# Which engine issues half of the second pass's loads: GpSimd in place of ScalarE, in a graph kernel that reads an 8192 x 8192 matrix twice

## The chip, the cores and the metric

One core of one Trainium2 chip runs the whole kernel. The metric is device time in microseconds (us) of one execution; lower is better. A profile is one further execution, recorded by the hardware profiler. Its durations are those of single instructions as that execution had them. Engines are TensorE (PE), VectorE (DVE), ScalarE (ACT), GpSimd (POOL) and SyncE (SP); a q behind the name (ACTq) is the engine's instruction queue, where DMA issues are seen.

## The reference

```python
x = layernorm(x + (1 - 0.1*x - 0.01 * sum(x * (adj @ x), axis=1)))      # first layer, x is 8192 x 64
A  = adj - diag(diag(adj))                                             # adj is 8192 x 8192 float32
node_support = concat([(A > 0) @ h, (A < 0) @ h])                       # h is the new x
edge_output  = gru_cell(node_support, h, ...)
att = softmax(where(A > 0, e_plus, -9e15) ...)                          # by rows; needs counts and sums of the positive entries
node_output  = gru_cell((att * A) @ (h @ W), h, ...)
out = layernorm(h + diag(adj) * edge_output + diag(adj) * node_output)
```

`adj` is sparse in its values (most entries are zero, the rest positive), but it is stored and read as a dense matrix of 268 MB. The first layer needs one pass over it, the second layer another, since `h` of all rows must be known before any row of the second layer can be done.

## The kernel before

**First pass.** SP streams `adj` in strips of 128 rows x 2048 columns (1 MB each) into a ring of 8 slots in SBUF; PE makes the Gram products, DVE multiplies and sums them (L610), ACT counts signs (L506). Every eighth tile a group of 1024 rows of `h` is finished; it goes to `h_rows` in DRAM and comes back in another layout as `hk` (`store_rows` L267, `rows_back` L276). The last group is finished in the seam between the passes by DVE, in steps that stand between its first transposes (`SEAM`).

**Second pass.** There are K = 16 blocks of 512 rows. A block is read as U = 8 units of 2 MB, and the same ring serves as 4 slots of one unit each (`SLOTS`). A unit is loaded by four DMAs, one for each group g of 32 partitions (`load_unit`, L247): partitions 32g to 32g+31 get columns 2048g + 256u to 2048g + 256u + 255 of the 512 rows. So one DMA moves 512 KB in 512 pieces of 1 KB, 32 pieces for each of the 16 DMA engines. Groups 0 and 1 (partitions 0 to 63) are issued by SP, groups 2 and 3 (partitions 64 to 127) by ACT; for units 0 to 3 of block 0 SP issues all four.

When the four DMAs of a unit have landed, POOL sets the diagonal of `adj` in it to zero (`no_diagonal`, L719). Then DVE transposes it in two halves (L806, `turned`), ACT takes the signs of each half (L932, `mask`, `mask_ready`), and PE multiplies: `weigh` (L1033) with the values, `add` (L1045) with the signs, in pairs of halves. The slot is free as soon as DVE has turned the second half. SP waits for that semaphore alone. ACT comes to its two DMAs in program order, behind the sign of the second half.

The small work of block k-1 (sums, softmax, gates, layer norm, store) is spread over the halves of block k: lists `AT` on each engine say at which half a step stands. On DVE `weighed_sum` (L813) stands at half 3 and `added_sum` (L818) at half 4, `reset` (L853) at half 10, the variance at 15 and `result` (L887) at 16. PE can't begin `weigh` of half 0 of a block before L813, nor `add` of half 0 before L818, since these steps empty its accumulators. POOL does the square root of the layer norm (`power`, L767) after the eighth `no_diagonal` of a block. ACT's steps are at halves 1, 2, 5, 6, 9, 10 and 16, among them three DMAs of 128 KB for each block (L946, L950, L989).

The order on POOL between the passes: it waits for `hk`'s first half, makes the high and low parts of it (L428, L430), and then comes to the first `no_diagonal`.

Of the kernel before, what the change touches and what calls it, by code (L numbers as in the profile page):

```python
# [6 lines left out]
Q = 32  # L7
G = P // Q
# [36 lines left out]
def build_gnn(nc, x, adj, w_gat, a_gat, w_ih_e, w_hh_e, b_ih_e, b_hh_e, w_ih_n, w_hh_n, b_ih_n, b_hh_n, out):  # L45
    N = adj.shape[0]
    GQ = N // G
    C = GQ // Q
    NB = N // P
    assert N % 8192 == 0 and x.shape[1] == D  # L50


    STRIP = 4 * BANK
    SPT = N // STRIP
    RING = 8
    TPB = RING // SPT
    LNG = 8
    GROUPS = C // LNG
    GC = C // 2
    XG = C // 4  # L60


    K = N // BANK
    UC = 8
    U = C // UC
    SLOTS = 4
    HC = UC // 2
    MS = 4
    H = 2 * U
    RB = BANK // Q  # L70


    scratch = nc.dram_tensor("h_rows", (N, D), F32, kind="Internal").ap()
    stack = ExitStack()

    def sem(name):
        return stack.enter_context(nc.semaphore(name))

    def keep(name, shape, dt):
        return stack.enter_context(nc.sbuf_tensor(name, shape, dt))  # L80

    with stack:

        hk = keep("hk", [P, C, D], F32)
        parts = keep("parts", [P, C, 2, D], F32R)
        ring = keep("ring", [P, RING, STRIP], F32)


        at = keep("at", [P, 4, HC, BANK], F32)
        mask = keep("mask", [P, MS, HC, BANK], F32R)
        final = keep("final", [P, 8, BANK], F32)
        ps = stack.enter_context(nc.psum_tensor("ps", [P, 8, BANK], F32))

        ones = keep("ones", [P, P], F32R)
        one = keep("one", [P, 1], F32)
        ident = keep("ident", [P, P], F32)
        flag = keep("flag", [1, 1], I32)
        a12 = keep("a12", [D, 2], F32)  # L100
        wie = keep("wie", [P, 2, 3, D], F32)
        whh = keep("whh", [D, 3, 2 * D], F32)
        w2 = keep("w2", [P, 3, D], F32)
        w_edge = keep("w_edge", [P, 2, D], F32)
        w_node = keep("w_node", [P, 2, D], F32)
        va = keep("va", [P, 2, 2], F32)
        pick = keep("pick", [P, 1], F32)
        two = keep("two", [P, D], F32)
        dnat = keep("dnat", [P, NB], F32)
        bias = keep("bias", [P, 2, 3], F32)  # L110
        brz = keep("brz", [P, 2], F32)
        bhn = keep("bhn", [P, 1], F32)
        not_diag = keep("not_diag", [P, K + U // 2 - 1, Q], F32)
        power = keep("power", [P, LNG], F32)
        keep_x = keep("keep_x", [P, 1], F32)
        lsum = keep("lsum", [P, 4, LNG], F32)


        count = keep("count", [P, C], F32)
        some = keep("some", [P, C], F32)  # L120
        off = keep("off", [P, C], F32)
        zeros = keep("zeros", [P, C], F32)
        dsign = keep("dsign", [P, C], F32)
        nat = keep("nat", [P, 4, D], F32)
        stage = keep("stage", [P, 4, D], F32)
        en = keep("en", [P, 4, 4], F32)
        co = keep("co", [P, 8, 4, 3], F32)
        prob0 = keep("prob", [P, 4, D], F32)
        seen = keep("seen", [P, K * H], F32)
        seen_k = keep("seen_k", [P, K], F32)  # L130
        count_k = keep("count_k", [P, K], F32)
        miss = keep("miss", [1, K + 1], F32)
        ls = keep("ls", [P, 4, 4], F32)


        xn = final[:, :, :].rearrange("p a m -> p (a m)").rearrange("p (c d) -> p c d", d=D)
        x2 = mask[:, :, :, :].rearrange("p s c i -> p (s c i)")
        slot_view = [at[:, i, :, :].rearrange("p c i -> p (c i)") for i in range(4)]
        pair = parts[:, C - 4:C, :, :].rearrange("p c e d -> p (c e d)").rearrange("p (t e m) -> p t e m", t=2, e=2)
        wstage = slot_view[0][:, 4 * P:4 * P + 23 * D].rearrange("p (a d) -> p a d", d=D)  # L140
        signs = slot_view[1].bitcast(BF16).rearrange("p (t m) -> p t m", t=2)
        wT = slot_view[2][0:D, 0:2 * D].rearrange("p (a d) -> p a d", d=D)
        wihn = slot_view[2][0:D, 2 * D:5 * D].rearrange("p (t d) -> p t d", d=D)
        sq = slot_view[3][:, 0:LNG * D].rearrange("p (c d) -> p c d", d=D)
        outer = slot_view[3][:, 512:512 + C * SPT].rearrange("p (c s) -> p c s", s=SPT)
        rowsign = slot_view[3][:, 1024:1024 + C * SPT].rearrange("p (c s) -> p c s", s=SPT)


        hT, tr, tz, hn, nn = (final[:, i, :] for i in (0, 3, 4, 5, 6))
        sums = [final[:, 1, :], at[:, 2, 0, :]]  # L150
        wsum = [final[:, 2, :], at[:, 2, 1, :]]
        y = final[:, 7, 0:4 * D].rearrange("p (b d) -> p b d", d=D)
        yo = final[:, 7, 4 * D:8 * D].rearrange("p (b d) -> p b d", d=D)
        prob = [prob0, at[:, 2, 2, 0:4 * D].rearrange("p (b d) -> p b d", d=D)]
        ysq = hn[:, 0:4 * D].rearrange("p (b d) -> p b d", d=D)
        cnt = [tr, tz]
        lows = nn

        s_carry = sem("carries_waits")
        s_nd = sem("not_diag_made")  # L160
        s_scr = sem("h_stored")
        s_hk = [sem("h_back_even"), sem("h_back_odd")]
        s_hi = [sem("high_first_half"), sem("high_second_half")]
        s_lo = [sem("low_first_half"), sem("low_second_half")]
        s_counts = sem("counts_ready")
        s_dsign = sem("diagonal_signs")
        s_raw = {prefix: [sem(f"{prefix}unit_loaded{i}") for i in range(SLOTS)] for prefix in ("f_", "g_")}
        s_miss, s_missed, s_flag = sem("misses_by_row"), sem("misses"), sem("flag_made")

        b = dict(locals())  # L170
        one_pass(nc, b)
# [67 lines left out]
                full.vector(dve)  # L239


def load_unit(eng, b, prefix, k, u, groups=(0, 1, 2, 3)):

    RB, UC, GQ, slot = b["RB"], b["UC"], b["GQ"], u % b["SLOTS"]
    raw = unit_view(b, slot).rearrange("p (f m) -> p f m", f=RB)
    for g in groups:
        eng.dma_start(  # L247
            raw[Q * g:Q * g + Q, :, :],
            b["adj"][bass.ds(k * BANK, BANK), GQ * g + UC * Q * u:GQ * g + UC * Q * (u + 1)].rearrange(
                "(f ii) m -> ii f m", ii=Q)).then_inc(b["s_raw"][prefix][slot], 16)  # L250


def unit_view(b, slot):
# [49 lines left out]
class First:  # L303
# [22 lines left out]
    def sync(self, sp):  # L326
# [26 lines left out]
        for u in range(b["SLOTS"]):  # L353
            sp.wait_ge(s["gram_free"], 2 + C * SPT - RING + 2 * (u + 1))
            sp.wait_ge(s["signs_summed"], C * SPT - RING + 2 * (u + 1))
            load_unit(sp, b, "f_", 0, u)


    def load_weights(self, pool):
# [352 lines left out]
def no_diagonal(nc, pool, b, prefix, k, u):  # L712

    U, UC, SLOTS = b["U"], b["UC"], b["SLOTS"]
    raw = unit_view(b, u % SLOTS)[:, (u % 2) * UC * (UC * Q):(u % 2 + 1) * UC * (UC * Q)]
    diag = bass.AP(tensor=raw.tensor, offset=raw.offset, ap=[list(raw.ap[0]), [UC * Q + Q, UC], [1, Q]])
    pool.wait_ge(b["s_raw"][prefix][u % SLOTS], (k * (U // SLOTS) + u // SLOTS + 1) * (16 * G))
    carry(pool, b["s_carry"])
    return nc.gpsimd.tensor_tensor(  # L719
        out=diag, in0=diag,  # L720
        in1=b["not_diag"][:, bass.ds(k + (U // 2 - 1 - u // 2), 1), :].to_broadcast([P, UC, Q]), op=ALU.mult)
# [6 lines left out]
class Fast:  # L728
# [33 lines left out]
    def gpsimd(self, pool):  # L762
        nc, b, s = self.nc, self.b, self.s

        def power(k):
            pool.wait_ge(s["variance_ready"], k + 1)
            nc.gpsimd.tensor_tensor(out=b["ls"][:, 3, :], in0=b["ls"][:, 2, :], in1=b["power"][:, 0:4],  # L767
                                    op=ALU.pow).then_inc(s["rstd_ready"], 1)

        def block(k, first):  # L770
            for u in range(self.U):
                no_diagonal(nc, pool, b, "f_", k, u).then_inc(s["diagonal_out"], 1)
                if first and u == 1:
                    self.first.last_power(pool)

        block(0, True)
        self.first.count_rows(pool)
        with pool.Fori(1, self.K) as k:
            block(k, False)
            power(k - 1)  # L780
        power(self.K - 1)


# [132 lines left out]
    def scalar(self, act):  # L916
# [8 lines left out]
        def sign(k, half, first, last):  # L925
            n = k * H + half
            act.wait_ge(s["turned"], n + 1)
            if not (first and half < MS):
# [4 lines left out]
                b["mask"][:, half % MS, :, :].rearrange("p c i -> p (c i)"),  # L933
                b["at"][:, half % 4, :, :].rearrange("p c i -> p (c i)").bitcast(U32), ACT.Sign,
                accum_out=b["seen"][:, bass.ds(n, 1)]).then_inc(s["mask_ready"], 1)
            u = half // 2 + SLOTS
            if half % 2 == 1 and (u < U or not last):
                load_unit(act, b, "f_", k + u // U, u % U, (2, 3))

        def staged_rows(k, first):  # L940

# [535 lines left out]
```

## Time and profile before

| | |
|---|---|
| median of 3 runs | 1680.99 us (1678.02 to 1808.76) |
| the profiled execution | 1673.49 us, of which 1671.7 us from the first instruction to the last |
| second pass | from about 695 us; TensorE starts block 0 at 698 us |
| moved by DMA | 550.18 MB, mean 329 GB/s |
| PE, DVE, ACT, POOL busy | 86%, 82%, 70%, 11% of the span |

The profile gives busy time of engines, not whether that work was in the way of the end. What one stage is limited by is read from who waits for whom in that stage, and from what a queue or an engine does in the gaps.

### The profile page before, as it was taken

Reading aid. Unit: us, or ns where it says so; the run is one execution under the profiler, and the core shown is the slowest. Engines: PE = TensorE matmul, PEld = TensorE weight load, DVE = VectorE, ACT = ScalarE, POOL = GpSimd, SP = SyncE. Lnnn points to the kernel's source line nnn. Section 1 sums busy time; section 2 is a strip of 40 time slices with the busy share of each in tenths; the row PEclk is TensorE's granted clock in tenths of the full one; section 3 lists DMA queues with packets and bytes.
Section 4 is the critical chain, followed back from the end, with each engine's and each line's share of the span. In section 5 each row is a group of like instructions: output and inputs, shape, how many; then the busy total and the mean of one; then the engine's idle time right before and its main releaser. Section 6 shows DMA issues by size and latency. Waiting matters only on the chain.

```text
span 1671.7 us, 22680 instructions
## 1 busy us (share of the span) xinstructions
PE 1445.0 (86%) x6262; PEld 794.9 (48%) x6262; DVE 1368.0 (82%) x1335; ACT 1163.8 (70%) x1409; POOL 178.0 (11%) x226
## 2 busy tenths in 40 slices
PE   7987878887888888558998899899999899999995
PEld 6655656555555555224444444444444444444442
DVE  5999899898989898647878877887788788778874
ACT  6987979797979797436666666666566666666662
POOL 2000000000001010201101111110111011111100
PEclk9999999999999999779999999999999999999996
DMA  9999999999999999999999999999999999999980
GB/s 264 418 421 422 410 422 409 421 410 421 411 421 413 419 413 419 233 200 333 303 288 306 292 293 296 308 288 291 299 305 298 299 302 295 297 300 310 293 215 11
DMA packets 366090, 550.18 MB, mean 329 GB/s; under 512 B 71024, under 2 KB 333184, under 8 KB 333296
## 3 DMA queue, kind: packets, MB, share of 16 engines
q1 hardware_dynamic: 190672, 408.49, 70.5%
q10 hardware_dynamic: 174976, 141.05, 33.1%
q0 software_dynamic: 416, 0.36, 0.1%
q8 instruction: 7, 0.11, 0.0%
q14 instruction: 19, 0.16, 0.0%
HBM read 545.66 MB, written 4.19 MB: 329 GB/s over the span
## 4 chain that ended last, share of the span: by engine, by line
DMA 30%; issue 21%; ACTq 15%; DVE 15%; PE 9%; ACT 7%; SPq 2%; DVEq 1%; POOL 0%; POOLq 0%
DMA ring<-in_adj 18%; ACTq L247 12%; DMA h_rows<-final 11%; DVE at L806 7%; DVE ps L610 5%; ACT mask L932 5%; PE ps L572 5%; SPq L247 2%; PE ps L1033 2%; ACTq L950 1%; PE ps L539 1%; ACTq L946 1%; PE ps L1045 1%; ACTq L989 0%; ACT final L970 0%
## 5 line engine op out<-in xcount | busy, mean ns | idle before, releaser
L932 ACT ACTIVATE mask<-at 128x2048 fp32r<-128x2048 uint32 x256 | 489.4, 1913 | 281.2 <-DVE at L806 189.6
L572 PE MATMUL ps<-mask,parts 128*128 128x512 f32 x2048 | 552.0, 413 | 101.9 <-DVE ps L610 68.2
L610 DVE SCALAR_TENSOR_TENSOR ps<-ring,ps 128x2048 f32<-128x2048 f32 x256 | 584.3, 2301 | 55.3 <-PE ps L572 34.8
L806 DVE STREAM_TRANSPOSE at<-ring 128x2048 f32<-128x2048 f32 x256 | 577.8, 2290 | 43.6 <-POOL ring L719 37.9
L1033 PE MATMUL ps<-at,hk 128*64 128x512 f32 x2048 | 495.6, 620 | 79.7 <-DVE final L813 42.3
L506 ACT ACTIVATE at<-ring 128x2048 bf16<-128x2048 f32 x256 | 488.7, 1909 | 97.0 <-DMA ring<-in_adj 52.5
L572 PEld LDWEIGHTS ps<-mask,parts 128*128 128x128 f32 x2048 | 374.9, 193 | 278.8 <-DVE ps L610 203.8
L1033 PEld LDWEIGHTS ps<-at,hk 128*64 128x64 f32 x2048 | 148.7, 141 | 346.1 <-issue 250.8
L1045 PE MATMUL ps<-mask,parts 128*128 128x512 f32 x1024 | 270.2, 405 | 13.6 <-ACT final L959 12.9
L1045 PEld LDWEIGHTS ps<-mask,parts 128*128 128x128 f32 x1024 | 182.1, 188 | 152.1 <-issue 73.4
L719 POOL TENSOR_TENSOR ring<-ring,not_diag 128x256 f32<-128x256 f32 x128 | 93.8, 733 | 715.0 <-DMA ring<-in_adj 715.0
L853 DVE SCALAR_TENSOR_TENSOR final<-final 128x512 f32<-128x512 f32 x16 | 11.1, 692 | 94.9 <-ACT final L976 89.7
L411 POOL TENSOR_TENSOR at<-at,lsum 128x512 f32<-128x512 f32 x7 | 7.3, 1045 | 435.2 <-DVE lsum L627 435.2
L506 ACT ACTIVATION_READ_ACCUMULATOR at<-ring 128x1 f32 x256 | 48.0, 188 | 0.0
L932 ACT ACTIVATION_READ_ACCUMULATOR mask<-at (+1 forms) x256 | 47.9, 187 | 0.0
L959 ACT COPY final<-ps 64x512 f32<-64x512 f32 x16 | 9.3, 583 | 47.1 <-issue 45.7
L818 DVE TENSOR_TENSOR final<-ps,final 64x512 f32<-64x512 f32 x16 | 10.9, 683 | 35.5 <-ACT final L959 35.5
L610 DVE DVE_READ_ACCUMULATOR ps<-ring,ps (+1 forms) x256 | 36.3, 142 | 0.0
L1079 PE MATMUL ps<-final,w_edge 128*64 128x512 f32 x64 | 35.4, 635 | 0.0
L1080 PE MATMUL ps<-final,w_node 128*64 128x512 f32 x64 | 35.4, 635 | 0.0
L767 POOL TENSOR_TENSOR ls<-ls,power 128x4 f32<-128x4 f32 x16 | 16.2, 1010 | 144.9 <-DVE ls L882 144.9
L968 ACT COPY final<-ps 128x512 f32<-128x512 f32 x16 | 9.4, 587 | 29.0 <-issue 29.0
(152 smaller groups left out, 645.4 us busy)
## 6 DMA issues: line engine op xcount, KB each, us to landing
ring<-in_adj SPq DMA_DIRECT2D x256, 1024.0 KB, 16.2
ring<-in_adj SPq DMA_DIRECT2D x264, 512.0 KB, 10.7
ring<-in_adj ACTq DMA_DIRECT2D x248, 512.0 KB, 14.3
stage<-h_rows ACTq DMA_DIRECT2D x16, 128.0 KB, 16.3
nat<-h_rows ACTq DMA_DIRECT2D x16, 128.0 KB, 15.8
out<-final ACTq DMA_DIRECT2D x16, 128.0 KB, 15.4
h_rows<-final ACTq DMA_DIRECT2D x7, 256.0 KB, 22.7
hk<-h_rows ACTq DMA_DIRECT2D x7, 256.0 KB, 23.9
```

The source lines that it names most:

```text
L247: eng.dma_start(raw[Q * g:Q * g + Q, :, :], b["adj"][bass.ds(k * BANK, BANK), GQ * g + UC * Q * u:GQ * g + UC * Q * (u + 1)].rearrange("(f ...
L506: nc.scalar.activation(signs[:, unit % 2, :], ring[:, unit % RING, :], ACT.Sign, accum_out=row_signs[:, unit:unit + 1]).then_inc(s["signs_ ...
L539: last = nc.tensor.matmul(ps[D * half:D * half + D, q % 4, P * i:P * i + P], xn[:, 4 * q + i, :], ident[:], start=True, stop=True, skip_gr ...
L572: last = nc.tensor.matmul(ps[:, 4 * (n % 2) + i, :], pair[:, t % 2, e, :], x2[:, cols], start=e == 0, stop=e == 1)
L610: nc.vector.scalar_tensor_tensor(out=gram, in0=ring[:, i % RING, :], scalar=1.0, in1=gram, op0=ALU.mult, op1=ALU.mult, accum_out=flat[:, b ...
L719: return nc.gpsimd.tensor_tensor(out=diag, in0=diag, in1=b["not_diag"][:, bass.ds(k + (U // 2 - 1 - u // 2), 1), :].to_broadcast([P, UC, Q ...
L806: nc.vector.transpose(b["at"][:, half % 4, :, :].rearrange("p c (f q) -> p f c q", q=Q), raw[:, :, HC * part:HC * part + HC, :]).then_inc( ...
L932: nc.scalar.activation(b["mask"][:, half % MS, :, :].rearrange("p c i -> p (c i)"), b["at"][:, half % 4, :, :].rearrange("p c i -> p (c i) ...
L1033: last = mm(o, h[:, c, :], b["at"][:, half % 4, cl, :], start=c < 2, stop=c >= H * HC - 2)
L1045: last = mm(ps[:, ACC_S, :], parts[:, c, :], b["mask"][:, half % MS, cl, :], start=c == 0, stop=c == H * HC - 1)
L1079: mm(ps[lo, bank, :], b["w_edge"][:, t, :], sums, start=True, stop=True)
L1080: mm(ps[hi, bank, :], b["w_node"][:, t, :], wsum, start=True, stop=True, skip_group_check=True).then_inc(s["gates"], 1)
```

## The change

GpSimd issues groups 2 and 3 of every unit of the second pass, those of units 0 to 3 of block 0 included. Their completion counts on semaphores of their own (`s_pooled`). GpSimd's order in a block becomes: `no_diagonal(u)`, then a wait until unit u-1 has been turned by DVE, then the two DMAs of unit u+3, then `no_diagonal(u+1)`. The two DMAs leave ACT's program (`sign`). SP issues only groups 0 and 1, of the first four units too. For those four GpSimd issues its eight DMAs in a row before the first `no_diagonal`, but behind the high and low parts of `hk`. The last block is written out apart from GpSimd's loop, so that nothing is loaded behind the matrix's end.

```diff
-def load_unit(eng, b, prefix, k, u, groups=(0, 1, 2, 3)):
+def load_unit(eng, b, prefix, k, u, groups=(0, 1, 2, 3), loaded=None):
+    loaded = loaded or b["s_raw"][prefix]
...
-                "(f ii) m -> ii f m", ii=Q)).then_inc(b["s_raw"][prefix][slot], 16)
+                "(f ii) m -> ii f m", ii=Q)).then_inc(loaded[slot], 16)
...
@@ First.sync, the first four units
-            load_unit(sp, b, "f_", 0, u)
+            load_unit(sp, b, "f_", 0, u, (0, 1))
...
@@ no_diagonal
-    pool.wait_ge(b["s_raw"][prefix][u % SLOTS], (k * (U // SLOTS) + u // SLOTS + 1) * (16 * G))
+    turn = k * (U // SLOTS) + u // SLOTS + 1
+    if prefix == "f_":
+        pool.wait_ge(b["s_raw"][prefix][u % SLOTS], turn * (16 * 2))
+        carry(pool, b["s_carry"])
+        pool.wait_ge(b["s_pooled"][u % SLOTS], turn * (16 * 2))
+    else:
+        pool.wait_ge(b["s_raw"][prefix][u % SLOTS], turn * (16 * G))
...
@@ Fast.gpsimd
-        def block(k, first):
+        def upper(k, u):
+
+            load_unit(pool, b, "f_", k, u, (2, 3), b["s_pooled"])
+
+        def block(k, first, last=False):
             for u in range(self.U):
                 no_diagonal(nc, pool, b, "f_", k, u).then_inc(s["diagonal_out"], 1)
+                v = u + b["SLOTS"] - 1
+                if (not first or u) and (v < self.U or not last):
+                    pool.wait_ge(s["turned"], k * self.H + 2 * u)
+                    carry(pool, b["s_carry"])
+                    upper(k + v // self.U, v % self.U)
                 if first and u == 1:
                     self.first.last_power(pool)
 
+        strips = self.first.UNITS * b["GROUPS"] - b["RING"]
+        for u in range(b["SLOTS"]):
+            pool.wait_ge(self.first.s["gram_free"], 2 + strips + 2 * (u + 1))
+            pool.wait_ge(self.first.s["signs_summed"], strips + 2 * (u + 1))
+            upper(0, u)
         block(0, True)
         self.first.count_rows(pool)
-        with pool.Fori(1, self.K) as k:
+        with pool.Fori(1, self.K - 1) as k:
             block(k, False)
             power(k - 1)
+        block(self.K - 1, False, True)
+        power(self.K - 2)
         power(self.K - 1)
...
@@ Fast.scalar, sign
-            u = half // 2 + SLOTS
-            if half % 2 == 1 and (u < U or not last):
-                load_unit(act, b, "f_", k + u // U, u % U, (2, 3))
```

## Rows read from the trace of the kernel before

**Rows 1.** The page: busy time by engine, GB/s in 40 slices of 41.8 us

```profile
PE 1445.0 (86%) x6262; PEld 794.9 (48%) x6262; DVE 1368.0 (82%) x1335; ACT 1163.8 (70%) x1409; POOL 178.0 (11%) x226
...
GB/s 264 418 421 422 410 422 409 421 410 421 411 421 413 419 413 419 233 200 333 303 288 306 292 293 296 308 288 291 299 305 298 299 302 295 297 300 310 293 215 11
```

**Rows 2.** Stretch A:B, length, busy PE PEld DVE ACT POOL, PEclk, DMA share, GB/s

```profile
1220.00:1340.00 120.00, 111.64 (x522) 52.20 (x521) 97.29 (x95) 76.76 (x87) 14.42 (x19) 1.00 1.11 297
```

**Rows 3.** Who waited for whom, 860 to 1580 us: us in total, times, longest

```profile
POOL ring L719 <- DMA ring<-in_adj: 539.8, 88, 9.8
...
DVE final L853 <- ACT final L976: 77.2, 13, 7.1
...
PE ps L1033 <- DVE final L813: 32.8, 12, 2.8
...
PE ps L1045 <- ACT final L959: 9.7, 6, 1.9
```

**Rows 4.** Instructions in order of time, ACT and DVE, 1319 to 1331 us

```profile
1322.38 2.87 ACTq L247 DMA_DIRECT2D ring<-in_adj  x1
1325.49 1.91 ACT L932 ACTIVATE mask<-at 128x2048 fp32r<-128x2048 uint32 x1 [4.29 <-issue]
...
1328.86 0.69 DVE L853 SCALAR_TENSOR_TENSOR final<-final 128x512 f32<-128x512 f32 x1 [6.80 <-ACT final L976]
```

**Rows 5.** Instructions in order of time, PE, a block's end and start

```profile
1352.84 1.09 PE L1054 MATMUL ps<-ident,stage 128*64 128x128 f32 x16
1356.76 5.07 PE L1033 MATMUL ps<-at,hk 128*64 128x512 f32 x16 [2.83 <-DVE final L813]
```

**Rows 6.** POOL's power step, once a block: ns min/median/max, first and last start

```profile
L767 POOL TENSOR_TENSOR ls<-ls,power x15: 1007/1009/1027, 825.0 to 1633.4; 128x4 f32<-128x4 f32 x15
```

**Rows 7.** Two short stretches of second pass: busy PE, PEclk, DMA share, GB/s

```profile
756.00:762.00 6.00, 6.00 (x28) 1.00 1.10 348
...
1335.00:1339.00 4.00, 4.00 (x23) 1.00 1.12 194
```

**Rows 8.** DMA queues (packets, MB, share) in 690:702, then 712:718, then 764:780

```profile
q1 hardware_dynamic: 2531, 2.51, 102.7%
...
q1 hardware_dynamic: 754, 0.74, 67.0%
q10 hardware_dynamic: 528, 0.53, 45.3%
...
q1 hardware_dynamic: 2783, 2.77, 55.2%
q10 hardware_dynamic: 2786, 2.77, 54.9%
```

**Rows 9.** DMA queue and issues in the first pass, 60 to 640 us

```profile
q1 hardware_dynamic: 32732, 238.42, 99.3%
...
h_rows<-final ACTq DMA_DIRECT2D x7, 256.0 KB, 22.7
```

**Rows 10.** GpSimd's own DMAs: at the start, and their queue over the span

```profile
2.55 2.45 POOL L365 DMA_DIRECT2D at<-in_L_gnn_w_ih_e  x4
...
q0 software_dynamic: 416, 0.36, 0.1%
```

**Rows 11.** Instructions in order of time in the seam, SP and POOL

```profile
670.13 47.61 SPq L247 DMA_DIRECT2D ring<-in_adj  x16
717.79 4.83 SPq L267 DMA_DIRECT2D h_rows<-final  x1
...
686.98 4.50 POOL L430 TENSOR_TENSOR parts<-hk,parts 128x2048 fp32r<-128x2048 f32 x1
...
719.61 0.72 POOL L719 TENSOR_TENSOR ring<-ring,not_diag 128x256 f32<-128x256 f32 x1 [12.41 <-DMA ring<-in_adj]
736.67 0.72 POOL L719 TENSOR_TENSOR ring<-ring,not_diag 128x256 f32<-128x256 f32 x1 [16.34 <-DMA ring<-in_adj]
```

**Rows 12.** The costliest groups of the page: DVE's transposes

```profile
L806 DVE STREAM_TRANSPOSE at<-ring 128x2048 f32<-128x2048 f32 x256 | 577.8, 2290 | 43.6 <-POOL ring L719 37.9
```

## The prediction on record

> **What bounds the kernel now.** I began with the page [rows 1]. The first pass moves 410 to 422 GB/s, the second about 300; GpSimd is busy for 11%. Since the change touches the second pass alone, the rest is read there. One block takes (1633.4 - 825.0) / 14 = 57.7 us [rows 6], a unit 7.21 us. In a steady stretch TensorE is busy for 93% [rows 2]. The view of waits says where the other 7% is: TensorE stands for L813 for 32.8 us in twelve blocks and for L959 (it lets L818 begin) for 9.7 us [rows 3], together 3.5 us a block. Both are at a block's start [rows 5]; between them TensorE runs without a gap. VectorE is late there because it was held earlier: 77.2 us in 13 blocks before L853, for ScalarE's tanh steps [rows 3]. In the timeline ScalarE isn't computing then: a load is issued from 1322.38 for 2.87 us, and the next sign starts 4.29 us late with "issue" as its reason; L853 comes 6.80 us late behind it [rows 4]. So ScalarE's two load issues a unit are in the way of the end, at 3.5 us a block. GpSimd does wait for loads, but VectorE hardly waits for GpSimd: the loads arrive in time, if not by much.
>
> **What the DMA rate hangs on.** This decides the case, and it isn't in the averages. With both queues active the engines move 348 GB/s at one time [rows 7]. At 1335 us it is 194. From 690 to 702 us one queue alone moves 2.51 MB in 12 us, 209 GB/s. One could take that for the limit of one queue. But from 712 to 718 us two queues are well filled and together move 1.27 MB in 6 us, 212 GB/s, while from 764 to 780 us two equally filled ones move 5.54 MB in 16 us, 346 GB/s [rows 8]. What differs is the destination. In the seam SP was at groups 2 and 3 of unit 2 (its diagonal step starts at 719.61, right behind them [rows 11]), and ScalarE's queue held groups 2 and 3 of unit 4. At 764 us SP carries groups 0 and 1, ScalarE's queue 2 and 3. So I read: 64 partitions take some 210 GB/s, and 346 needs both halves fed at once. A block brings each half 8.39 MB: 40 us at 210 GB/s, so that a half is idle for at most 17 us of 57.7.
>
> How do two queues share an engine? The shares of two full queues sum to 110% [rows 8]: an engine serves nearly one packet at a time. And they take turns by packets, not by bytes: in the first pass q1 carries 8 KB pieces, 0.993 x 16 x 580 us over 29,100 of them (32,732 packets less some 3,600 completions of 227 loads), or 317 ns each. Beside it a store of 256 KB in 1024 pieces, 64 for an engine, takes 22.7 us, 355 ns a piece [rows 9]: one 8 KB packet of the other queue and 38 ns for itself.
>
> Now both queues of the second pass make a packet of each 1 KB piece. One packet costs an engine 16 x 16 us / 5569 = 46 ns with both halves fed, and 16 x 12 us / 2531 = 76 ns with one half alone [rows 8]. Turn and turn about, both halves get the same.
>
> **GpSimd's queue makes bigger packets.** Its 13 DMAs at the start left 416 packets, 32 each, two for an engine [rows 10]. The four of L365 have 48 KB in 192 pieces of 256 B, twelve for an engine. One of the two packets must be the completion, so twelve pieces of together 3 KB went in one packet. That is the lower bound of a packet's size here; the upper one is the whole 32 KB that an engine has of a 512 KB DMA. The Trainium skill ("DMA: Bandwidth & Descriptors", section "SWDGE vs HWDGE vs iDMA") gives a size for it: at most 4096 B preferably and 64 descriptors. The trace shows neither limit; with four pieces a packet the sum below would have some 9.0 us a unit in place of 8.8.
>
> **The change, part by part.**
>
> (1) ScalarE loses two issues a unit. The cost removed is the 3.5 us a block of TensorE's waits, by 15 blocks 53 us at most. It is worth that only if the loads follow: a block of 54.2 us needs 17.2 MB (297 GB/s by 57.7 us [rows 2, 6]), 317 GB/s. ScalarE's own work is 36 us a block, so nothing new appears on it.
>
> (2) GpSimd gains two issues a unit. Four with 192 pieces took 2.45 us, 0.61 us each [rows 10]. No row has 512 pieces: at least 0.61 if it is a fixed cost, at most 0.61 x 512 / 192 = 1.63 us if all of it goes by pieces. I take 1.1. GpSimd then has 0.73 + 2.2, at most 4.0 us in 7.2 us of a unit. It stays off the path. Queued behind the issues is the next `no_diagonal`, with VectorE behind it; the new wait (unit u-1 turned) is met about when the diagonal of u is out. The root of the layer norm stands behind one such pair, and its variance comes more than a transpose later. Cost nothing while an issue takes less than about 3 us. The loads start earlier than ScalarE's by its sign, 2 us or more, which helps nothing if the engines are the limit. A rule of the skill speaks against this: VectorE's fast two-port modes keep GpSimd from writing descriptors ("SBUF — State Buffer", section "Who interferes with whom"). VectorE's transposes take 2290 ns for 2048 elements a partition, 1.1 ns each [rows 12], which isn't a fast mode; so I put it at nothing.
>
> (3) The sharing of the engines. A unit brings 1.05 MB to each half, 64 pieces of 1 KB per engine. While GpSimd's packets last, they go at their half's rate: 1.05 MB / 210 GB/s = 5.0 us. In turn with them SP gets one 1 KB packet for each. At 3 KB that is 21 of its 64, at no time of their own at best, at 46 ns each (1.0 us) at worst. The other 43 go alone at 76 ns: 3.3 us. Sum 8.3 to 9.3 us. With 32 KB packets it is 5.0 + 62 x 76 ns = 9.7 us. The shares of 110% allow a tenth off: 7.5 us at best. I take **8.8 us a unit**, the middle of the 3 KB case, because that is the size nearest to a row; against 7.21 now it is +1.59 us, by the 124 units behind the first four +197 us. Then SP's queue is the bound, the 3.5 us of (1) lie within its waiting and bring nothing, and TensorE waits some 16 us a block.
>
> (4) The seam. SP's 16 issues last from 670.13 to 717.8 us, and `store_rows` stands behind them; unit 3 is complete at 736.67 [rows 11]. After: SP has eight, some 20 us of one half, done near 692. GpSimd can begin only behind L430, at 691.5 [rows 11], alone on its half: 4.2 MB / 210 = 20 us, unit 3 at about 712. Its eight issues delay the first diagonal step by 5 to 13 us, against 695 now. The store can leave when VectorE's L686 is done, 3 to 7 us earlier, and has less before it. VectorE's first eight halves should end 9 to 24 us earlier. The store's way back is behind them in length, so I take -15, range -20 to -5.
>
> (5) New semaphores, waits and the last block written out: a tenth of a us each beside GpSimd's idle time, nothing.
>
> Sum against the profiled execution's own time: 1673.5 + 197 - 15 = 1855.5. The median of the runs is 7.5 us above it; I add that: **1863 us**. By the bounds: 7.5 us a unit gives 1673.5 + 36 - 20 + 7.5 = 1697, 9.8 us gives 1673.5 + 321 - 5 + 7.5 = 1997.
>
> **Rivals.**
>
> *B, the engines stay fair, ScalarE's time is won.* Either GpSimd's packets are single pieces when these are 1 KB, or an engine goes on with SP's queue while GpSimd's packet is held at its half. Then 346 GB/s or more are there, against 317 needed, and TensorE is the bound: 1673.5 - 53 - 15 + 7.5 = 1613, range 1600 to 1635. For it: rows 3 and 4, which are certain. Against it: 12 pieces in a packet, and 355 ns a piece beside 8 KB packets. It decides as soon as a unit's loads take less than 6.8 us.
>
> *C, about even.* The same sharing, but with enough overlap that a unit takes 6.9 to 7.5 us. Gain in the seam and loss later nearly cancel: 1640 to 1700.
>
> *D, GpSimd is the bound.* The mechanism: writing 512 descriptors takes it longer than thought, since no row shows that many. From 3.9 us an issue, GpSimd's 0.73 + 2 x 3.9 + 0.3 us pass 8.8 us a unit. With 5.5 us a unit takes 12 us: 1673.5 + 124 x 4.8 = 2270. Against it: 0.61 us for 192 pieces.
>
> *E, it doesn't do what it says:* GpSimd's DMAs would have to come out on a hardware queue. They have their own, q0 [rows 10]. No chance given.
>
> **Chances.** Forecast (7.5 to 9.8 us a unit, 1697 to 1997) 0.68; B 0.16; C 0.12; D 0.04. Faster by over 2% (below 1647; 2% is about what a measurement of this kernel can tell from no change): B and a little of C, 0.17. Within 2% (to 1715): the rest of C and the low end of the forecast, 0.14. Slower: 0.69. The range of 1640 to 1990 holds the forecast's case nearly whole and C; B is left out. The forecast's own range is 1700 to 1990.
>
> **What the changed profile would show.** Right: blocks of about 70 us by the power step; GB/s that swing between about 270 and 210 within each unit, with q0 near its half's rate in short bursts and q1 alone in between; SP's loads taking over 20 us to land, GpSimd's 5 to 6; VectorE waiting for the diagonal step. q0 with packets far fewer than 512 for a load. In both outcomes: no "issue" waits of ScalarE before L932, L959 and L968, and L853 waiting for 3 us or less unless it is late itself; unit 3's diagonal near 712 us. GpSimd's DMA rows at 0.6 to 1.6 us each. Wrong: landings of both queues about equal and blocks of 54 us (B), or GpSimd busy for most of a unit (D). The step that I trust least is (3), that an engine stands still for SP while GpSimd's packet is held.

## The result, and the profile after

| | |
|---|---|
| after, median of 4 runs | 1888.18 us (1882.58 to 1889.97) |
| before, median of 4 runs beside them | 1681.35 us (1678.02 to 1808.76) |
| ratio | 1.1232, 95% interval 1.1198 to 1.1266: slower |
| the profiled execution after | 1889.97 us, span 1888.3 us |

Under one and the same code the kernel before took 1668.5 to 1692 us in some executions and 1699 to 1813 us in the others; every ratio here is against the first of these, run beside the changed kernel, and the change lies above both.

The page after the change: busy time, then GB/s in 40 slices of 47.2 us.

```profile
PE 1494.7 (79%) x6262; PEld 808.5 (43%) x6262; DVE 1379.9 (73%) x1335; ACT 1170.9 (62%) x1409; POOL 348.9 (18%) x482
...
GB/s 268 422 422 411 422 411 422 412 416 416 413 421 413 422 268 205 239 241 237 241 238 238 240 240 239 239 236 239 242 239 237 243 235 239 238 242 238 239 223 10
```

Against [rows 1] the first pass is as it was, and the second runs at 240 GB/s in place of 300. GpSimd is busy for 171 us more, in 256 DMA rows. So look for what lowers the DMA rate, while no engine comes near being full. The steady stretch, the waits (860 to 1780 us) and the power step once a block, which answer to [rows 2], [rows 3] and [rows 6]:

```profile
1220.00:1340.00 120.00, 100.80 (x432) 45.17 (x434) 80.19 (x79) 64.25 (x74) 27.73 (x40) 0.91 1.09 239
```

```profile
POOL ring L727 <- DMA ring<-in_adj: 637.3, 102, 11.5
...
DVE at L830 <- POOL ring L727: 251.8, 76, 7.8
...
PE ps L1054 <- DVE final L837: 127.8, 13, 12.7
...
DVE final L877 <- ACT final L997: 16.7, 13, 1.3
```

```profile
L775 POOL TENSOR_TENSOR ls<-ls,power x15: 1033/1038/1046, 844.8 to 1849.4; 128x4 f32<-128x4 f32 x15
```

A block takes (1849.4 - 844.8) / 14 = 71.76 us, a unit 8.97 us against 7.21. Read the waits from the top: GpSimd waits for loads, VectorE for GpSimd's diagonal step (37.9 us in the whole pass before [rows 12]), TensorE for VectorE at a block's start. That is a chain behind the DMAs. 124 units x 1.76 us = 218 us, and the two profiled executions differ by 1889.97 - 1673.49 = 216.5 us: the whole loss is in the steady rate.

Queues, GpSimd's DMA rows and the landings on the page, then the same queues in the steady stretch:

```profile
q1 hardware_dynamic: 186448, 404.29, 71.5%
q0 software_dynamic: 37280, 134.60, 28.3%
...
L249 POOL DMA_DIRECT2D ring<-in_adj x256 | 170.0, 668 | 35.5 <-DVE at L830 17.0
...
ring<-in_adj SPq DMA_DIRECT2D x256, 512.0 KB, 22.3
ring<-in_adj POOLq DMA_DIRECT2D x256, 512.0 KB, 10.9
```

```profile
GB/s 238 264 263 253 242 256 217 198 198 245 268 266 248 221 263 231 198 214 272 255 256 234 226 202 247 261 263 247 231 266 221 198 200 257 260 259 241 201 245 253
...
q1 hardware_dynamic: 13501, 13.41, 57.2%
q0 software_dynamic: 4030, 14.67, 48.1%
```

37,280 packets are 416 of the start and 36,864 = 256 x 144. With 16 completions a DMA that leaves 128 for 512 KB: **4096 bytes a packet**. The Trainium skill ("DMA: Bandwidth & Descriptors", section "SWDGE vs HWDGE vs iDMA") gives this size as the preferred most for a packet of GpSimd's path, and here the trace agrees.

The decisive rows are two stretches of 3 us within one unit, first 1303 to 1306, then 1306 to 1309:

```profile
q1 hardware_dynamic: 534, 0.53, 90.7%
q0 software_dynamic: 33, 0.13, 21.1%
```

```profile
q0 software_dynamic: 171, 0.63, 80.9%
q1 hardware_dynamic: 170, 0.17, 25.9%
```

While GpSimd's burst lasts, **171 packets of one queue stand against 170 of the other**, and these move 0.63 MB (210 GB/s, its half's full rate) against 0.17 MB (57 GB/s). In the other stretch SP's queue is nearly by itself, at 178 GB/s. That is why the rate swings between 198 and 272 and is never near the 348 of [rows 7].

The seam, SP and then GpSimd, in order of time, which answers to [rows 11]:

```profile
671.87 22.13 SPq L249 DMA_DIRECT2D ring<-in_adj  x8
719.66 0.41 SPq L269 DMA_DIRECT2D h_rows<-final  x1
...
739.69 0.31 SPq L278 DMA_DIRECT2D hk<-h_rows  x1
```

```profile
693.27 5.29 POOL L249 DMA_DIRECT2D ring<-in_adj  x8
707.09 0.72 POOL L727 TENSOR_TENSOR ring<-ring,not_diag 128x256 f32<-128x256 f32 x1 [8.53 <-DMA ring<-in_adj]
...
725.86 0.73 POOL L727 TENSOR_TENSOR ring<-ring,not_diag 128x256 f32<-128x256 f32 x1 [2.00 <-DMA ring<-in_adj]
...
743.20 0.72 POOL L727 TENSOR_TENSOR ring<-ring,not_diag 128x256 f32<-128x256 f32 x1 [15.02 <-DMA ring<-in_adj]
```

SP has its eight loads issued by 694, but its store leaves at 719.66, for VectorE finishes the last rows only then: the first diagonal step is at 707.09, since GpSimd's loads began at 693.27. The store takes 20 us to come back (719.66 to 739.69), as it did before (717.79 to 738.66). Unit 3 is 11 us earlier than in [rows 11], but unit 4 isn't: GpSimd waits 15.02 us for it and has it at 743.20, against 742.11 before.

### The profile page after: what moved, and what is told of

Read it like the earlier page. It is cut to its first block, busy times and chain, and to the rows that moved or that the text cites. A ratio compares the mean times of both kernels' runs of the same rounds, so it can differ in the third digit from the quotient of the medians.

```text
span 1888.3 us, 23042 instructions
## 1 busy us (share of the span) xinstructions
PE 1494.7 (79%) x6262; PEld 808.5 (43%) x6262; DVE 1379.9 (73%) x1335; ACT 1170.9 (62%) x1409; POOL 348.9 (18%) x482
## 3 DMA queue, kind: packets, MB, share of 16 engines
q0 software_dynamic: 37280, 134.60, 28.3%
## 4 chain that ended last, share of the span: by engine, by line
DMA 52%; SPq 15%; DVE 11%; issue 11%; PE 8%; POOL 1%; ACT 1%; DVEq 0%; POOLq 0%; ACTq 0%
DMA ring<-in_adj 42%; SPq L249 15%; DMA h_rows<-final 8%; DVE ps L612 6%; PE ps L574 5%; DVE at L830 4%; DMA hk<-h_rows 2%; PE ps L1054 1%; POOL ring L727 1%; PE ps L541 1%; PE ps L1066 0%; PE ps L1114 0%; DMA final<-in_x 0%; ACT at L508 0%; ACT parts L476 0%
## 5 line engine op out<-in xcount | busy, mean ns | idle before, releaser
L1054 PE MATMUL ps<-at,hk 128*64 128x512 f32 x2048 | 533.0, 659 | 218.7 <-DVE final L837 147.7
L1054 PEld LDWEIGHTS ps<-at,hk 128*64 128x64 f32 x2048 | 156.7, 150 | 515.1 <-issue 273.7
L249 POOL DMA_DIRECT2D ring<-in_adj x256 | 170.0, 668 | 35.5 <-DVE at L830 17.0
L1114 PE MATMUL ps<-two,final 128*128 128x64 f32 x128 | 20.3, 311 | 19.7 <-DVE final L886 19.7
L1114 PEld LDWEIGHTS ps<-two,final 128*128 128x128 f32 x128 | 19.3, 225 | 24.7 <-DVE final L886 24.2
## 6 DMA issues: line engine op xcount, KB each, us to landing
ring<-in_adj SPq DMA_DIRECT2D x256, 512.0 KB, 22.3
ring<-in_adj POOLq DMA_DIRECT2D x256, 512.0 KB, 10.9
```

Of the source, the lines that this page charges most:

```text
L249: eng.dma_start(raw[Q * g:Q * g + Q, :, :], b["adj"][bass.ds(k * BANK, BANK), GQ * g + UC * Q * u:GQ * g + UC * Q * (u + 1)].rearrange("(f ...
L1054: last = mm(o, h[:, c, :], b["at"][:, half % 4, cl, :], start=c < 2, stop=c >= H * HC - 2)
L1114: last = mm(ps[:, MISC, D * q:D * q + D], b["hT"][:, P * q:P * q + P], b["two"][:, :], start=True, stop=True)
```

## Experiments

**Is it the packets' size? The changed kernel with SP's packets as big as GpSimd's.** For groups 0 and 1 a unit reads other columns of the same rows, so that a piece is 4 KB:

```diff
+    flat = unit_view(b, slot).rearrange("p (f m) -> p f m", f=4)
+            eng.dma_start(flat[Q*g:Q*g+Q, :, :],
+                b["adj"][bass.ds(k*BANK + P*(u//2), P), GQ*g + 1024*(u%2):GQ*g + 1024*(u%2+1)]
+                    .rearrange("(f ii) m -> ii f m", ii=Q)).then_inc(loaded[slot], 16)
-    ... b["ps"][0:1, HN, 0:K], 0.0, None, ALU.not_equal)
+    ... b["ps"][0:1, HN, 0:K], -1e30, None, ALU.is_lt)
```

> The changed kernel, but SP's loads (groups 0 and 1) take pieces of 4 KB in place of 1 KB: the same bytes of the same block, in another order within the unit. What it leaves out: the unit's entries stand in another order, so the sums are of permuted data, and the comparison of counts behind the second pass never asks for the fallback. Theory (engines take turns by packets, GpSimd's packets are 4 KB, and they hold up SP's 1 KB packets): both queues are equal again, over 340 GB/s in the second pass, blocks of 54 to 55 us instead of 71.8, total about 1888 - 15.5 x 17 = 1625 us (1600 to 1650). Rival 1 (GpSimd's program order: a load waits behind the diagonal step and the turn of the unit before): blocks stay near 71 us, 1870 to 1890. Rival 2 (DMAs whose descriptors GpSimd writes are slow in themselves): GpSimd's loads still take about 11 us to land and blocks stay at 65 to 71 us, 1790 to 1880.

Measured: 1629.11 us (profiled) and 1674.19 us, of which the first alone is within the theory's range. The steady stretch and its queues:

```profile
1220.00:1340.00 120.00, 116.77 (x548) 55.11 (x545) 106.29 (x110) 82.89 (x94) 39.88 (x56) 1.00 1.04 321
```

```profile
q0 software_dynamic: 5163, 18.79, 52.3%
q1 hardware_dynamic: 5156, 18.77, 47.4%
...
ring<-in_adj SPq DMA_DIRECT2D x36, 512.0 KB, 16.6
ring<-in_adj POOLq DMA_DIRECT2D x36, 512.0 KB, 16.2
```

Equal packets give equal bytes and equal landings, 321 GB/s, and TensorE busy for 97%; a block takes (1584.7 - 824.6) / 14 = 54.3 us. Nothing that GpSimd does was changed. So its issues, its new waits and its order cost next to nothing by themselves (54.2 us was worked out for a block with no such cost), and the loss hangs on the size of the other queue's pieces.

**The same unequal sizes without GpSimd.** The kernel before, with 4 KB pieces for groups 2 and 3 from ScalarE's queue; the edit is the one above with `g in (2, 3)`.

> The kernel before, GpSimd issues nothing in the second pass, but ScalarE's loads (groups 2 and 3), and groups 2 and 3 of the first four units, take 4 KB pieces; SP's stay at 1 KB. What it leaves out: entries of groups 2 and 3 stand in another order, and the fallback is never asked for. Theory (packet size by itself): this is the changed kernel's traffic without GpSimd. A unit takes 5.0 us for the large packets of one half and 48 x 76 ns for SP's other packets, 8.7 to 9.3 us, blocks of 70 to 74 us, total 1860 to 1920 us. Rivals 1 and 2 (the loss comes from GpSimd's order or from its way of writing descriptors): ScalarE's issues get cheaper with a quarter of the pieces, so it is faster than before, 1620 to 1660 us.

Measured: 1873.53 us (profiled) and 1859.41 us, ratio 1.115 (1.0967 to 1.1334).

```profile
q1 hardware_dynamic: 14261, 14.16, 58.1%
q10 hardware_dynamic: 6042, 14.82, 50.1%
...
ring<-in_adj SPq DMA_DIRECT2D x28, 512.0 KB, 21.0
ring<-in_adj ACTq DMA_DIRECT2D x28, 512.0 KB, 12.2
```

SP's landings (21.0 us), the rate (241 GB/s) and the block (70.6 us) are close to those of the change (22.3 us, 239 GB/s, 71.76 us). Unequal packets are enough.

**Both queues with 4 KB, ScalarE issuing.** The kernel before with `g in (0, 1, 2, 3)`.

> The kernel before with 4 KB pieces in all loads of the second pass, ScalarE issuing as before. What it leaves out: as in the two others (entries in another order, no fallback). Shows what the loads are worth when they are no limit. Theory: the two queues are equal, over 350 GB/s are there, ScalarE's issues no longer fill its queue, TensorE is the bound: blocks of 54 us, 1600 to 1640 us. Rival (the loads are already no limit before, only the issue is): the same time. Rival (HBM gives no more than 300 GB/s in this order of reading): 1660 to 1690 us, blocks stay at 57.

Measured: 1773.19 us (profiled) and 1825.38 us, 64.1 us a block: the forecast failed. The waits (860 to 1580 us) and ScalarE in order of time:

```profile
ACT final L966 <- issue: 98.9, 11, 11.1
```

```profile
1275.18 10.90 ACTq L249 DMA_DIRECT2D ring<-in_adj  x1
...
1288.13 0.58 ACT L966 COPY final<-ps 64x512 f32<-64x512 f32 x1 [10.80 <-issue]
```

One load's issue holds ScalarE for 10.90 us, in each block before the same step: 9 us a block. In the kernel before, this step (L959 there) waited for ScalarE's issues 3.1 us a block:

```profile
ACT final L959 <- issue: 36.7, 12, 4.2
```

Against the first experiment it differs mainly in who issues groups 2 and 3. With equal packets GpSimd as issuer is thus the better one by 9.8 us a block in these two executions. That the idea of the change is sound and its packets spoil it rests on this and on the first experiment, neither of which gives the kernel's own output.

**Does the rate hang on both halves being fed?** The kernel before; SP issues groups 0 and 2, ScalarE 1 and 3.

```diff
-load_unit(sp, b, "f_", k, u, (0, 1))
+load_unit(sp, b, "f_", k, u, (0, 2))
-load_unit(act, b, "f_", k + u // U, u % U, (2, 3))
+load_unit(act, b, "f_", k + u // U, u % U, (1, 3))
```

> The kernel before, complete, but SP issues groups 0 and 2 and ScalarE groups 1 and 3, so that each queue goes to both halves of the partitions in turn. Theory (64 partitions take about 210 GB/s, 346 needs both halves at once, whichever queue): the heads of the queues are in the same half about half of the time, (210 + 346) / 2 = 278 GB/s or less against 297 used, blocks of 60 to 64 us, 1715 to 1780 us. Rival (210 GB/s is what one queue of 1 KB pieces gives, 346 what two give): no difference, 1675 to 1690 us.

Measured: 1925.70 to 1951.32 us (4 runs), ratio 1.1624 (1.1529 to 1.1719); the effect has the sign expected, but a block takes 74.8 us where 60 to 64 were expected: 17 us more than before, not 2 to 6. The steady stretch:

```profile
1220.00:1340.00 120.00, 93.42 (x394) 42.08 (x390) 71.29 (x72) 55.60 (x64) 9.74 (x13) 0.89 1.13 226
```

```profile
q10 hardware_dynamic: 15525, 13.45, 56.4%
q1 hardware_dynamic: 13798, 13.70, 56.2%
```

Two full queues with equal packets make 226 GB/s, near what one half takes (209 to 212 in [rows 8]). Then the same with ScalarE's pair turned round, `(3, 1)`, so that the queues start in opposite halves:

> As e4_before_mixed_halves, with one difference: ScalarE's queue issues group 3 first and then group 1, in place of 1 and then 3. SP's stays at 0 and then 2. So each queue still writes to both halves in turn, but when SP is in partitions 0 to 63 ScalarE's queue is in 64 to 127, and the other way about. Output complete. Theory (the rate hangs on both halves being fed at the same time; in e4 both queues were in the same half, since both started low and equal packets keep them in step): the step is now opposite, 300 to 350 GB/s for much of the time, and the time falls from e4's 1926 towards the kernel before: 1670 to 1810 us, 58 to 64 us a block; the upper part if ScalarE's stalls push the two into the same half at times. Rival 1 (a queue that changes halves is slow in itself, or the alternation costs): about as e4, 1900 to 1950 us, 226 GB/s. Rival 2 (the two queues find the same half again whatever the start, since the one that is alone in a half runs ahead): 1850 to 1950 us, with short stretches of 346 GB/s at a unit's start only.

Measured: 1825.68 us median (1818.16 to 1847.75, 4 runs), 117 us below the median of the last by the order of two issues alone.

```profile
1220.00:1340.00 120.00, 105.01 (x463) 48.56 (x463) 85.61 (x78) 67.91 (x78) 12.96 (x17) 0.95 1.12 268
```

It is 16 us above the theory's range and 74 us below the least of rival 1's: a queue that changes halves need not be slow. Slices between 210 and 323 GB/s fit queues that drift into the same half part of the time (rival 2 in a mild form); no row here follows the queues by halves.

**One queue for all 128 partitions.** SP alone, one DMA for each f over all groups, no load on ScalarE:

```diff
+    for f in range(RB):
+        eng.dma_start(raw[:, f, :],
+            b["adj"][bass.ds(k*BANK + Q*f, Q), :].rearrange("ii (g c) -> g ii c", g=4)
+                [:, :, UC*Q*u:UC*Q*(u+1)]).then_inc(b["s_raw"][prefix][slot], 16)
```

> The kernel before, but SP alone loads a unit, in 16 DMAs of 128 KB, one for each set of 32 rows (the index f of the tile): each writes one piece of 1 KB to every one of the 128 partitions, so both halves are fed by one queue at all times. ScalarE issues no load in the second pass, GpSimd none. Output complete. Theory (64 partitions take some 210 GB/s at 76 ns a packet, both halves together 346 GB/s at 46 ns; a queue as such is no limit): the loads could take 6.0 us a unit, ScalarE's issue stalls are gone, TensorE is the bound with 54 us a block: 1610 to 1640 us, GB/s about 315 in the second pass. That holds if SP can issue 16 DMAs in 6.8 us (0.42 us each); the shortest issue of a 512 KB load on a hardware queue was 0.32 us. If an issue takes 0.6 us, SP is the bound with 9.6 us a unit: about 1970 us. Rival (one queue of 1 KB pieces is limited to some 210 GB/s whatever it writes to): a unit takes 10 us, 80 us a block, about 2010 us, with SP's loads landing late and its issues held by a full queue.

Measured: 3563.76 us, which neither theory had. SP in order of time, then the DMAs of 1246 to 1252 us:

```profile
1234.58 26.09 SPq L248 DMA_DIRECT2D ring<-in_adj  x19
```

```profile
DMA packets 582, 0.58 MB, mean 96 GB/s; under 512 B 18, under 2 KB 582, under 8 KB 582
...
q1 hardware_dynamic: 582, 0.58, 27.2%
```

A DMA takes 26.09 / 19 = 1.37 us and the engines are 27% busy. The 18 small packets are completions; the other 564 are 4.4 DMAs of 128 pieces, so a DMA has four completions, not 16: it went to four engines. The Trainium skill ("DMA: Bandwidth & Descriptors", section "Why a DMA increments its semaphore by 16 and not by 1") has the rule: the largest number up to 16 that divides the slowest dimension of both sides, here the four groups of the source. The trace agrees, with four completions. The run says nothing on whether one queue can feed both halves.

**Seam alone and steady part alone.** First GpSimd issues groups 2 and 3 of units 0 to 3 of block 0, and ScalarE the rest as before; then the reverse, SP issuing all of the first four units and GpSimd the upper groups of all others.

```diff
 seam alone:    for u in range(SLOTS): load_unit(pool, b, "f_", 0, u, (2, 3), b["s_pooled"])
                sign: load_unit(act, ..., (2, 3)) stays
 steady alone:  First.sync: load_unit(sp, b, "f_", 0, u)        # all four groups
                block: upper(k + v // self.U, v % self.U)       # as in the change
```

> Complete kernel. One part of the change alone: GpSimd issues groups 2 and 3 of the first four units, ScalarE those of all others as before. Theory (as the changed trace reads: unit 3 is there 11 us earlier, unit 0 12 us later, and the stored rows come back at 744 us as before, since the store takes 20 us to land beside 4 KB packets): TensorE's second half of block 0 starts at 745 to 750 us, total within 8 us of before, 1673 to 1689 us. My prediction's step (4) would have it 15 us faster, 1666 us. Rival (the late start of GpSimd behind the parts of hk costs): 10 us slower.

> Complete kernel. The other part alone: SP issues all groups of the first four units as before, GpSimd groups 2 and 3 of all units from the fifth on. Theory (the whole loss comes unit by unit from the packets): blocks of 71 to 72 us as in the changed kernel, total 1870 to 1895 us. Rival (the seam puts the two queues in a bad phase that then stays): blocks clearly shorter than 71 us, under 1850 us.

Measured, seam alone: 1743.5 to 1773.3 us (4 runs), ratio 1.0538 (1.0475 to 1.0601), 62.1 us a block. The forecast failed: from unit 4 on the same work is issued by the same engines as before, yet each block is 4.4 us longer. The first power step is 6 us later than before (831.3 against 825.0); the rest of the loss comes after it. Its waits (860 to 1700 us) show VectorE held behind ScalarE's tanh steps for longer than the 77.2 us in 13 blocks of [rows 3]:

```profile
DVE final L866 <- ACT final L989: 104.8, 14, 9.9
```

Steady alone: 1890.97 us (profiled) and 1881.94 us, ratio 1.1253 (1.1181 to 1.1324), as the whole change. The power step:

```profile
L776 POOL TENSOR_TENSOR ls<-ls,power x15: 1032/1037/1044, 844.7 to 1849.1; 128x4 f32<-128x4 f32 x15
```

71.74 us a block, and the first power step at 844.7 us where the whole change has 844.8: beside the rest of the change, its seam moves the time by nothing.

**Half the dose.** GpSimd issues group 3 alone, ScalarE group 2:

```diff
-load_unit(pool, b, "f_", k, u, (2, 3), b["s_pooled"])
+load_unit(pool, b, "f_", k, u, (3,), b["s_pooled"])
+load_unit(act, b, "f_", k + u // U, u % U, (2,))
```

> Complete kernel. GpSimd issues group 3 alone, ScalarE group 2, SP groups 0 and 1 (and group 2 of the first four units). Theory: GpSimd's 8 packets of 4 KB a unit and engine go with ScalarE's 1 KB for the same half, 3.1 us while SP gets 8 packets; then 24 pairs of 1 KB at 92 ns, 2.2 us; then 32 of SP alone, 2.4 us: 7.7 us a unit, blocks of 60 to 64 us, total 1720 to 1780 us, between before and changed. Rival (any load from GpSimd's queue is late in itself and holds the unit up): as slow as the changed kernel, 1860 to 1890 us.

Measured: 1766.22 us (profiled) and 1762.24 us, ratio 1.0523 (1.0482 to 1.0565), 63.7 us a block; landings 17.6 us for SP, 18.1 for ScalarE's, 9.2 for GpSimd's. That is within the theory's range and rules its rival out: a load from GpSimd's queue doesn't hold the unit up in itself. How much of the 6 us a block is owed to the big packets it doesn't say, for ScalarE still issues loads here, and the seam alone, with no big packet in the steady part, has 62.1 us a block.

**Can ScalarE's stalls be removed without GpSimd?** The kernel before, each of ScalarE's load pairs one or more halves later in its program (`LATER = {2: 1, 4: 3, 6: 5, 9: 7, ...}`: at half 2 the load of half 1, and so on), so that it finds its queue emptier.

> Complete kernel, all else as before: ScalarE's loads stay on ScalarE, but stand behind the steps of the next half (behind added_sum's copy at half 2, the state's at 6, the tanh at 10), and those of half 7 behind the gates at half 9. Theory (ScalarE stands while it issues, and only these steps pass that on to VectorE and TensorE): L853's wait of 6 us a block and TensorE's 3.5 us at the block's start get smaller, 15 to 45 us faster, 1635 to 1665 us. Rival (loads arrive with 0.2 to 5 us to spare, so loads issued 2 to 5 us later make VectorE wait for the diagonal step): no difference or up to 20 us slower.

Measured: 1779.02 to 1830.98 us (6 runs), ratio 1.0697 (1.0574 to 1.0821), 66.5 us a block. An issue of a load on ScalarE took 2.8 us in the median (800 to 1600 us), more than the 1.66 us before. So the stalls grew. No kernel here that gives the whole output was faster than the one before at its best.

## Why the prediction was right

It said 1863 us, slower, by packets of unequal size; 1888 was measured. By its steps:

- **(1) ScalarE's stalls.** They are gone: ScalarE waits for no issue, and VectorE waits for its tanh step 16.7 us in 13 blocks in place of 77.2 [rows 3]. As said, this is hidden by the loads. The first experiment shows what it is worth when these follow: 54.3 us a block, where 54.2 was worked out.
- **(2) GpSimd's issues.** 0.668 us each, where 1.1 was taken between 0.61 and 1.63. A DMA of 512 pieces costs nearly as one of 192 [rows 10], so the cost is all but fixed. They hide, as the first experiment shows.
- **(3) The sharing.** 8.8 us a unit was predicted, 8.97 measured, which is 21 us of the error of the sum. The turn-taking by packets is shown by 171 against 170. The packet is 4 KB, not 3: GpSimd's 1.05 MB take 5.0 us, in which SP gets 57 GB/s, 17 of its 64 pieces for each engine; the other 47 at 76 ns give 3.6 us, together 8.6; the last 0.4 us of a unit is in no row. The step trusted least (an engine stands for SP while GpSimd's packet is held at its half) holds: q1 gets 57 GB/s, though its own half is free.
- **(4) The seam** is the step that failed: -15 was predicted, and the first power step is 19.8 us later (844.8 against 825.0 in [rows 6]), of which 12 units of block 0 and 1 at 1.76 us explain 21.1: about -1. Neither the seam alone (6 us later) nor the whole change against the steady part alone (0.1 us later) shows a gain. Unit 3 was to be at 712 and was at 725.86; the store was to leave 3 to 7 us earlier and left 2 us later, since the first transposes started some 12 us late behind GpSimd's eight issues and loads. Its way back is as long as before (20.0 against 20.9 us), so the second half of block 0 could not start earlier: VectorE's step behind it is at 745.77, where it was at 744.77.
- **(5)** Nothing, as said.
- The sum: +34.5 us from (3) and (4), and -9.3 us since the profiled execution after lies 1.8 us above its median, not 7.5 below.

Rival B (fair engines) falls by the queue rows; C too, since two queues in a burst make 267 GB/s and not 300. D falls: GpSimd is busy 28 us in 120. GpSimd's landing was to be 5 to 6 us and is 10.9. Its burst does take 5 us, but it starts late: a pair is issued from 1327.93 to 1329.25, from 1330 to 1334 only SP's queue moves anything, and in 1334 to 1340 the pair's 1.05 MB follow. So a row of 0.67 us for an issue isn't the time until the data moves; what fills the 5 us between, no run shows. The queues in 1330 to 1334, then GpSimd's in 1334 to 1340:

```profile
q1 hardware_dynamic: 827, 0.82, 113.9%
...
q0 software_dynamic: 288, 1.05, 69.4%
```


The Trainium skill ("DMA: Bandwidth & Descriptors", section "Rules for kernel authors") says that spreading DMAs over SP, ScalarE and GpSimd brings no bandwidth and only saves issue time. The measurement differs: here the issue time was saved and 12% lost.

What stays open: why a small disturbance (the seam alone, later loads, 4 KB for both) leaves the kernel with ScalarE's issues in a longer course for the rest of the pass. I read it as a loop: a queue that is full holds ScalarE, its next load is late, one half is idle for that time, and the queues stay full. That is argued from the stalls and rates, and no run separates it. Nor is it shown that the edits did it: these times (1743 to 1831 us) lie within those that the kernel before itself took, 1668.5 to 1813 us, or little above. The main readings don't hang on this, for the change (1883 to 1890 us) and unequal packets without GpSimd (1859 and 1874 us) lie above all of them.

## What to carry to other kernels

DMA queues share an engine by packets, so the queue with the bigger packets takes the bytes: before a DMA is moved to another queue, work out the packet that each queue makes of its pieces, and change the sizes together. Then see which partitions each queue writes to at one time: here half of the partitions took some 210 GB/s, and the 346 GB/s of [rows 8] needed both halves fed at once. An issue that looks free can hold a compute engine for microseconds, but removing the hold pays only if the loads follow.

## What the runs showed of the hardware

- GpSimd's issue: 0.61 us for 192 pieces, 0.668 us for 512; the pair looked at above moved its first bytes some 5 us after its issues.
- An issue on ScalarE into a full queue: up to 10.90 us in the stretch shown.
- A DMA whose source is three-dimensional with 4 as its outermost size went to four engines: 1.37 us for 128 KB. The same bytes a unit took 22 us in place of 7.21.
- TensorE is slower behind a wait. In order of time, and the windows (granted clock in the third column from the end):

```profile
1349.46 6.13 PE L1054 MATMUL ps<-at,hk 128*64 128x512 f32 x16 [4.59 <-DVE at L830]
...
1368.34 5.23 PE L1054 MATMUL ps<-at,hk 128*64 128x512 f32 x16 [9.68 <-DVE final L837]
```

```profile
1350.00:1356.00 6.00, 6.00 (x18) 1.71 (x15) 5.97 (x6) 3.60 (x5) 3.15 (x4) 0.63 1.11 214
1368.00:1374.00 6.00, 5.66 (x18) 1.92 (x19) 5.14 (x4) 3.52 (x4) 2.05 (x3) 0.70 1.12 229
```

Sixteen matrix products took 6.13 and 5.23 us there, while eight of the same with no wait before them took 1.94 us at 1376.52. The clock was granted at 0.63 and 0.70 of full speed, that is partly at 1.2 and partly at 2.4 GHz. The loss doesn't follow the length of the wait: it was more behind 4.59 than behind 9.68 us. TensorE's busy time rose from 1445.0 [rows 1] to 1494.7 us for the same instructions.
